# A quantised cross-attention and mixture-of-experts block: rounding on ScalarE, paired maxima, queries stacked before keys

## The reference, cut to what matters

```python
def _qdq(x):                       # symmetric int8, one scale per row
    s = maximum(max(abs(x), axis=-1) / 127, 1e-8)
    return clip(round(x / s), -127, 127) * s

q = _qdq(layernorm(x)) @ _qdq(wq).T + bq
k, v = split(ctx @ wkv.T + bkv, 2)
attn = softmax(q @ k.T / sqrt(32))            # 16 heads, 512 x 1601 each
o = attn @ v
x = x + tanh(g0) * (_qdq(o) @ _qdq(wp).T + bp)
x = x + tanh(g1) * moe(layernorm(x))          # 32 experts, top 4, capacity 128,
                                              # plus a shared SwiGLU
```

## Time and profile before

| | |
|---|---|
| runs of the kernel, median (lowest to highest) | 3401.5 us (3399.94 to 3410.48) |
| the profiled execution | 3410.04 us, of which the span is 3408.1 us |
| mean granted TensorE clock | 0.912 of full speed |
| PE busy | 2915.5 us, 86% |
| DVE / ACT / POOL busy | 1958.9 us (57%) / 1265.7 us (37%) / 1826.3 us (54%) |
| setup and first maxima | 0 to 137 us |
| attention | 137 to about 2691 us |
| SwiGLU and routing | about 2691 to 3160 us |
| experts | 3160 to 3408 us |

### The profile page before, as it was taken

One profiled execution on the slowest core, in us unless ns is written; L12 is line 12 of the kernel. 1 busy time (PEld: TensorE's weight loads), 2 busy tenths in 40 slices (PEclk: granted clock), 3 DMA queues, 4 the chain that ended last, 5 costly groups with the idle time before them and its releaser, 6 DMA issues. The chain is left out here.

```text
span 3408.1 us, 43422 instructions
## 1 busy us (share of the span) xinstructions
PE 2915.5 (86%) x14836; PEld 1224.1 (36%) x14876; DVE 1958.9 (57%) x4052; ACT 1265.7 (37%) x2268; POOL 1826.3 (54%) x1570
## 2 busy tenths in 40 slices
PE   5997888888888887988798879888989879998787
PEld 3233333333333332333233333333333334443665
DVE  7667566756675667567666766675566143434122
ACT  2254435443544354445444534454345410100111
POOL 0285566456645575556465646564658613233555
PEclk9798999799979998998899979997999789999899
DMA  4111012110211031102110211121110221131897
GB/s 126 27 42 49 24 28 71 45 35 17 79 36 37 17 92 35 39 12 89 33 33 20 85 31 32 34 74 28 32 45 20 75 87 53 60 111 49 249 288 193
DMA packets 146651, 215.73 MB, mean 63 GB/s; under 512 B 25016, under 2 KB 78264, under 8 KB 146432
## 3 DMA queue, kind: packets, MB, share of 16 engines
q1 hardware_dynamic: 130560, 196.08, 19.1%
q0 software_dynamic: 15872, 16.87, 2.6%
HBM read 126.62 MB, written 34.37 MB: 47 GB/s over the span
## 5 line engine op out<-in xcount | busy, mean ns | idle before, releaser
L1439 POOL TENSOR_TENSOR prob_acc<-prob_acc,probs 128x512 f32<-128x512 f32 x1152 | 1449.4, 1289 | 614.4 <-ACT probs L965 614.1
L965 ACT ACTIVATE probs<-s_ps 128x512 f32<-128x512 f32 (+1 forms) x1664 | 942.9, 596 | 1091.6 <-PE s_ps L786 1060.9
L1184 DVE TENSOR_REDUCE piece_max<-r_ps 128x1 f32<-128x400 f32 (+1 forms) x2048 | 1025.2, 565 | 176.0 <-PE r_ps L708 172.6
L708 PE MATMUL r_ps<-k_flat,q_stack 96*128 96x400 f16 (+1 forms) x2048 | 637.4, 366 | 238.8 <-DVE piece_max L1184 138.2
L786 PE MATMUL s_ps<-q_stack,k_flat 97*128 97x512 f16 (+1 forms) x1664 | 649.8, 407 | 64.7 <-ACT probs L965 57.0
L800 PE MATMUL o_ps<-probs,v_sb 128*32 128x512 f32 (+1 forms) x3328 | 480.2, 651 | 19.8 <-ACT probs L965 19.8
L708 PEld LDWEIGHTS r_ps<-k_flat,q_stack 96*128 96x128 f16 x2048 | 205.1, 101 | 556.0 <-DVE piece_max L1184 268.4
L786 PEld LDWEIGHTS s_ps<-q_stack,k_flat 97*128 97x128 f16 (+1 forms) x1664 | 163.8, 103 | 645.6 <-ACT probs L965 389.6
L1436 POOL COPY prob_acc<-probs 128x512 f32<-128x512 f32 x128 | 72.8, 612 | 520.2 <-PE sum_ps L820 383.7
L1471 POOL DMA_INDIRECT slot_rows<-payload,slot x128 | 125.3, 979 | 315.0 <-DVE slot L1369 192.8
L1178 DVE SCALAR_TENSOR_TENSOR k_lo<-r_ps,bk_col,k_hi 128x400 f16<-128x400 f32 (+1 forms) x128 | 81.8, 639 | 333.2 <-ACT k_hi L923 333.2
(11 more groups left out here) (190 smaller groups left out, 2781.2 us busy)
## 6 DMA issues: line engine op xcount, KB each, us to landing
k_flat<-k_hi SPq DMA_DIRECT2D x256, 100.1 KB, 2.2
ctx_raw<-in_ctx SPq DMA_DIRECT2D x96, 256.0 KB, 2.7
v_sb<-in_L_ffn_w SPq DMA_DIRECT2D x48, 512.0 KB
xin<-in_x SPq DMA_DIRECT2D x16, 1024.0 KB, 5.5
k_flat<-k_lo SPq DMA_DIRECT2D x128, 100.1 KB, 2.2
ctx_hi<-in_L_ffn_w SPq DMA_DIRECT2D x24, 512.0 KB
ctx_lo<-in_L_ffn_w SPq DMA_DIRECT2D x24, 512.0 KB
q_stack<-q_hi SPq DMA_DIRECT2D x256, 32.0 KB, 1.9
```

Source lines behind the costliest of these rows:

```text
L708: last = nc.tensor.matmul(ps[:, 0:w], q_stack[0:KSPLIT, g % 2, j, qt * P:(qt + 1) * P], k_stack[0:KSPLIT, g % 2, j, at:at + w], start=True ...
L965: nc.scalar.activation(probs[0:w, slot, j, :], s_ps[j % SBANKS][0:w, :], ACT.Exp).then_inc(probs_ready, 1)
L1184: V.reduce_max(piece_max[:, j * TT + qt, i:i + 1], ps[:, 0:PIECE[i]], X_AXIS).then_inc(free_of(*key), 1)
L1439: last = G.tensor_tensor(prob_acc[:, j, :], prob_acc[:, j, :], probs[:, slot, j, :], ALU.add)
```

## The change

It has five parts.

1. **Normalising and rounding move to ACT.** `normalised` becomes `Identity(x * rstd + shift)`, `rounded` `Identity(x * inv + 12582912)`, `integers` subtracts it into bf16. VectorE keeps one pass, a clip between the last two, with both bounds. Two tiles go in a step. For x the statistics move to step 1, the deviation to 2, the scale stays at 6. For h, h_ready comes from ACT at steps 3 and 4.
2. **Maxima in pairs.** A `"max"` tile is now two matmuls into two neighbouring banks, read by one reduction over 2 x 401 or 2 x 400 columns. A pair starts at an even bank; where the tile before ended on an even one, a bank is skipped.
3. **Queries before keys** also where g=0: the `q` tile moves from step 1 to the lead of step 0, ahead of the first key piece, and SP copies queries first everywhere but at the very start.
4. **The row of maxima** goes by one DMA from `max_row` to `q_stack`.
5. At the start `x` is loaded after the first context tile, not the third.

```diff
-X_STATS, X_STD, X_NORM, X_SCALE, X_QUANT = 2, 3, 4, 6, 7
-O_SCALE, O_QUANT, O_TURN, Y_AT = 3, 4, 9, 10
-H_STATS, H_STD, H_NORM, LATE_HEADS = 0, 1, 2, 10
+X_STATS, X_STD, X_RSTD, X_NORM, X_SCALE, X_ROUND, X_CLIP, X_INT = 1, 2, 3, (4, 5), 6, (7, 8), (8, 9), (10, 11)
+O_SCALE, O_ROUND, O_CLIP, O_INT, O_TURN, Y_AT = 3, (4, 5), (5, 6), (7, 8), 9, 10
+H_STATS, H_STD, H_RSTD, H_NORM, LATE_HEADS = 0, 1, 2, (3, 4), 10
...
-    return (x_tiles(nb) if ng == 0 else [("q", nb, ng)]) + key_tiles(nb, ng)[0:2]
+    return (x_tiles(nb) if ng == 0 else []) + [("q", nb, ng)] + key_tiles(nb, ng)[0:2]
...
+        for key in order:
+            wide = 2 if key[0] == "max" else 1
+            at += at % wide
+            banks = [(at + i) % NBANKS for i in range(wide)]
+            at += wide
...
             def stacks(b, g):
 
-                if g == 0:
+                if (b, g) == (0, 0):
                     stack_keys(b, g, range(GH))
...
                 sp.wait_ge(max_row_ready, group(b, g) + 1)
-                sp.dma_start(max_scr[g % 2], max_row[:, :]).then_inc(max_out, DMA)
-                sp.wait_ge(max_out, (group(b, g) + 1) * DMA)
                 sp.dma_start(q_stack[KSPLIT:KSPLIT + 1, g % 2, :, :].rearrange("o j n -> o (j n)"),
-                             max_scr[g % 2].rearrange("(o a) n -> o (a n)", o=1)).then_inc(max_in, DMA)
+                             max_row[:, :]).then_inc(max_in, DMA)
...
+                    w = MAX_WIDE[i]
+                    open_tile(*key)
+                    for ps, at in zip(r_ps[ring.bank(*key):], MAX_AT[i]):
+                        last = nc.tensor.matmul(ps[:, 0:w], q_stack[0:KSPLIT, g % 2, j, qt * P:(qt + 1) * P],
+                                                k_stack[0:KSPLIT, g % 2, j, at:at + w], start=True, stop=True)
...
+            def normalised(dst, tiles, ready, count, done):
+
+                act.wait_ge(ready, count)
+                for t in tiles:
+                    nc.scalar.activation(dst[:, t, :], xin[:, t, :], ACT.Identity, scale=rstd[:, t:t + 1],
+                                         bias=shift[:, t:t + 1]).then_inc(done, 1)
+
+            def rounded(src, tiles, ready, count, done):
+
+                act.wait_ge(ready, count)
+                for t in tiles:
+                    nc.scalar.activation(src[:, t, :], src[:, t, :], ACT.Identity, scale=inv[:, t:t + 1],
+                                         bias=rounder[:, 0:1]).then_inc(done, 1)
+
+            def integers(src, tiles, ready, count, done):
+
+                for t in tiles:
+                    act.wait_ge(ready, count + t + 1)
+                    nc.scalar.activation(q_int[:, t, :], src[:, t, :], ACT.Identity, bias=rounder[:, 1:2]).then_inc(done, 1)
...
+            def clip_rows(src, tiles, ready, count, done):
+
+                for t in tiles:
+                    dve.wait_ge(ready, count + t + 1)
+                    V.tensor_scalar(src[:, t, :], src[:, t, :], ROUND + 127.0, ROUND - 127.0, ALU.min, ALU.max).then_inc(done, 1)
...
+                    full(dve, *key)
+                    k = ring.bank(*key)
+                    V.reduce_max(piece_max[:, j * TT + qt, 2 * i:2 * i + 2], r_all[:, k:k + 2, 0:MAX_WIDE[i]], X_AXIS
+                                 ).then_inc(free_of(*key), 1)
```

More of the change, by code:

```diff
@@ L34 @@
 PIECE_AT = [sum(PIECE[:i]) for i in range(PIECES)]
+PAIRS = PIECES // 2
+MAX_WIDE = [max(PIECE[2 * i:2 * i + 2]) for i in range(PAIRS)]
+MAX_AT = [(PIECE_AT[2 * i], PIECE_AT[2 * i + 1] + PIECE[2 * i + 1] - MAX_WIDE[i]) for i in range(PAIRS)]
 E, TOPK, EGROUPS, EPG, CAP, F, FS = 32, 4, 4, 8, 128, 256, 512
@@ L84, in max_tiles @@
 def max_tiles(b, g):
-    return [("max", b, g, j, qt, i) for j in range(GH) for qt in range(TT) for i in range(PIECES)]
+    return [("max", b, g, j, qt, i) for j in range(GH) for qt in range(TT) for i in range(PAIRS)]
 def x_tiles(b):
@@ L432, in full @@
         def full(eng, *key):
-            k = ring.bank(*key)
-            eng.wait_ge(bank_full[k], ring.done(*key))
-            return r_ps[k]
+            eng.wait_ge(bank_full[ring.last_bank(*key)], ring.done(*key))
+            return r_ps[ring.bank(*key)]
         def free_of(*key):
-            return bank_free[ring.bank(*key)]
+            return bank_free[ring.last_bank(*key)]
         def wait_read(eng, *key):
@@ L560, in ffn_in @@
                     key = ("hT", f - 2, DC - 1)
-                    sp.wait_ge(bank_full[ring.bank(*key)], ring.done(*key))
+                    sp.wait_ge(bank_full[ring.last_bank(*key)], ring.done(*key))
                     sp.wait_ge(out_written, (f - 1) * DMA)
@@ L606, in open_tile @@
             def open_tile(*key):
-                k = ring.bank(*key)
-                if ring.uses_before(*key):
-                    pe.wait_ge(bank_free[k], ring.uses_before(*key))
-                return r_ps[k]
+                for k, count in ring.before[key]:
+                    pe.wait_ge(bank_free[k], count)
+                return r_ps[ring.bank(*key)]
             def close(last, *key):
-                last.then_inc(bank_full[ring.bank(*key)], 1)
+                last.then_inc(bank_full[ring.last_bank(*key)], 1)
             pe.wait_ge(consts_ready, 1)
@@ L1001, in _ @@
                 tile(key)
+            for at in O_ROUND + O_INT:
+                o_part(B - 1, at)
             for f in range(B):
@@ L1131, in h_part @@
                     variances(h_var_ready)
-                elif at == H_NORM:
-                    inverse_std(h_std_ready, b + 1)
-                    for t in range(TT // 2):
-                        step.mark(normalised(work, t))
-                elif at == H_NORM + 1:
-                    for t in range(TT // 2, TT):
-                        last = normalised(work, t)
-                        if t < TT - 1:
-                            step.mark(last)
-                    last.then_inc(h_ready, 1)
+                elif at == H_RSTD:
+                    inverse_std(h_std_ready, b + 1, h_rstd_ready)
             def tile(key):
@@ L1232, in _ @@
             heads_out(B - 1, GROUPS - 1)
-            quantise(work, so).then_inc(o_quantised, 1)
+            for at in (O_SCALE,) + O_CLIP:
+                o_part(B - 1, at)
             def scores_in_groups():
@@ L1483, in gather @@
                 key = ("ey", e - UN) if e >= UN else ("down", B - 1, TT - 1)
-                pool.wait_ge(bank_full[ring.bank(*key)], ring.done(*key))
+                pool.wait_ge(bank_full[ring.last_bank(*key)], ring.done(*key))
                 step.carry_wait()
```

142 lines of the change are left out of this document (87 added, 55 removed).

## The result

| | before | after |
|---|---|---|
| median of the runs (lowest to highest) | 3404.01 us (3399.94 to 3410.48) | 3250.49 us (3247.85 to 3254.07) |
| ratio, 95% interval | | 0.9548 (0.9529 to 0.9567) |
| the profiled execution, its span | 3410.04, 3408.1 | 3254.07, 3251.4 |
| mean granted TensorE clock | 0.912 | 0.950 |
| PE / DVE / ACT busy, us | 2915.5 / 1958.9 / 1265.7 | 2811.8 / 1727.0 / 1387.3 |

The account below looks back on a forecast made before the run. PE was taken to bound attention, stopped mainly by VectorE at the maxima and returning at half clock. Terms 66 + 140 + 30 + 1 = 237 us off 3410 gave 3173, forecast as 3170; main case 3110 to 3240, range 3090 to 3300.

Parts of the forecast that it names:

- Pairs: Attention's maxima: one reduction over two banks saves 0.08 us a pair, seen in 20 groups and the start; about 30 us.
- The bound of -60: Lower bound for maxima in pairs: each remaining stop 0.45 us longer, and a bank skipped beside every single tile.
- The passes: Normalising and rounding off VectorE: 182 us gross, less 21 for clips and 21 on ACT; about 140 us.
- ScalarE's share, 21: The moved passes' cost on ACT, behind a step's fourth exponential: 3 us a batch, 21 in all; at worst 97.
- my 2.55 against 2.5: Before a step's first exponential ACT needs 2.55 us while PE has about 2.5 us of work: just covered, except in g=2.
- Queries first: Queries copied before keys in g=0: PE starts g=3's first query earlier, 9.4 us in each of 7 batches, 66 us.
- The rest: Direct copy of the maxima row and later h_ready in SwiGLU, with SwiGLU and experts unchanged: together +1 us.
- Statistics one step earlier: Statistics of x moved ahead of step 3: no gain, since PE then waits for a context tile; -3 to +3 us a batch.
- the one that ended slower: Rival: with two pair places PE and VectorE take turns, 3640 us; signs: reductions 0.98 us or more, over 40 waits; chance 0.05.
- ScalarE takes VectorE's place: Rival: uncovered ACT bursts hold PE, 3310 us; sign: `s_ps` waits for ACT above 15 us a batch; chance 0.13.
- The change does little: Rival: VectorE's stops return at the next maxima, 3320 us; sign: g=2 still near 90 us; chance 0.09.
- Everything goes: Rival: the clock stays up and stops at the scales shrink too, 20 us a batch more, 3090 us; chance 0.11.

Follow-up runs that it names:

- run 10: The kernel before with queries first and the direct copy of the maxima row; single maxima, all normalising and rounding on VectorE: 3358.44 us, ratio 0.9842.
- run 1: The changed kernel with maxima taken one bank at a time again, all else as changed: 3181.28 us, ratio 0.9323.
- run 6: The kernel with single maxima (3181 us), but the ring still skips a bank where a pair would have to: 3218.77 us, ratio 0.9439.
- run 7: The kernel with single maxima (3181 us), with the row of maxima sent through DRAM again: 3175.75 us, ratio 0.9303.
- Runs 9 and 11: 9: single-maxima kernel without ScalarE's square root, 3169.97 us. 11: single maxima, row maxima in halves, four context-tile places in place of three, 3121.6 us.
- run 8: The kernel with single maxima (3181 us), with the row maxima of x and o taken in two halves, one a step earlier: 3142.19 us, ratio 0.9218.

## Why the forecast was 80 us too low

The sum was 66 + 140 + 30 + 1 = 237. The measured 154 us are parted by the ratios in the same way: 54 for the order with the direct copy (before to run 10), 177 for the passes (run 10 to run 1), -77 for the pairs (run 1 to the changed kernel). By the medians as they stand the pairs are -69, because the kernel before was 8 us slower beside the runs than beside the changed kernel; I go on with 69, the smaller. (237 off the runs' own 3401.5 would have been 3165, not 3170; that is within the noise.)

**Pairs: the step that failed, 99 us of the sum.** "20 groups x 1.3, and 3 at the start, 29 in all" looked only at what the instruction saves. That part was too small: 49 us were measured. The other side stood beside it as the lower bound, "a pair gives its banks back only when both are read", "and a bank is skipped beside every single tile", and was not priced into the value taken. The runs show that it costs 37 + 81 = 118 us. The bound of -60 was not low enough either, since I charged the late return only to stops that already stood in the profile; the pairs made new ones, 28 a batch for 9 in run 1 with single maxima. The clock is not what was lost: it was 0.950 over the program for 0.948 in run 1, and PE is busy 7 us longer and idle 63. The Trainium skill, "TensorE: Matmul & The Clock Gate", "A second HAM failure mode", tells of a clock that swings because of short idles in a bank cycle. The short idles are there in the trace, but between run 1 and the changed kernel no clock was lost; of the runs between them run 6 alone shows longer busy time, at 0.943.

**The passes: 177 for 140.** The stops went as told: `piece_max` fell from 19.7 us a batch in run 10 to 5.9 in run 1, 13.8 where the sum had 14. (Of the six stops behind these passes five, and not six, are of 2 us or longer; the sixth is 1.63.) PE's idle time fell by 10.2 only, since waits for other things grew, that for a context tile by 1.8. Three sizes were off. The clock gave back 16.5 us of PE's busy time a batch, the loss by the clips already taken off, where 12 were taken. The clips cost 35 for 21. And ScalarE's share, 21, does not show: PE waits 6.8 us a batch for the exponentials in run 10 and 6.7 in run 1. ScalarE's passes are even longer than the 0.60 us I took from a row that reads PSUM (forms of after, ns min/median/max):

```profile
L942 ACT ACTIVATE xin<-xin,rounder,inv x32: 799/808/816, 59.2 to 2172.4; 128x512 f32<-128x512 f32 x32
...
L949 ACT ACTIVATE q_int<-xin,rounder x32: 708/718/728, 63.8 to 2189.2; 128x512 bf16<-128x512 f32 x32
```

So "it is just covered" was right by the result, but not by my 2.55 against 2.5: with the measured lengths the first would be 3.0. Why the cover is wider was not tried.

**Queries first: 53 to 56 for 66.** The mechanism is as told: the first query copy goes out long before the last `k_lo`, and PE starts 3.46 us after that has ended (SP, VectorE and PE in g=3 of after):

```profile
1583.10 1.15 SPq L517 DMA_DIRECT2D q_stack<-q_hi  x2
```

```profile
1594.40 0.64 DVE L1246 SCALAR_TENSOR_TENSOR k_lo<-r_all,bk_col,k_hi 128x400 f16<-128x400 f32 x1 [2.93 <-ACT k_hi L996]
```

```profile
1598.50 0.52 PE L732 MATMUL r_all<-k_flat,q_stack 96*128 96x401 f16 x2 [1.34 <-DMA k_flat<-k_hi]
```

But that `k_lo` ends 18.4 us into the group, and I had 17.2 us ("at about 1688"). PE starts 21.9 us into it for 28.6, so 6.7 us are gained and not 7.7. The granted clock of g=3 is 1.00, where it was 0.94.

**The rest.** The direct copy gives nothing that can be told from zero (run 7; 1 us was taken). Statistics one step earlier and the earlier load of x were not tried alone. Runs 9 and 11 show that the wait for a context tile behind the statistics is real: four places take it away and give 21 us.

**The rivals.** Of the one that ended slower, the mechanism is in the result: by its own mark, reductions at 0.98 us or more (986 ns), it is there, by the other, over 40 waits a batch, not fully (28). It costs 69 us, not 470; that a pair in flight and PE's other work cover the rest is my reading and was not tried. (Its 3640 also leaves the 30 us of pairs in; with them out it is 3670.) "ScalarE takes VectorE's place" is refuted by its own mark: 15 us a batch of waits for ScalarE were asked for, and it is 7.8 in the changed kernel. "The change does little" falls by g=2. "Everything goes" was half right for the scales: their stops can be cut (run 8), but don't go by themselves. Its price was also mistaken: 20 us a batch more would be about 3020, and 3090 needs only some 10. The measured 3250 lies in none of the cases as priced, above the 3110 to 3240 of the main one and below the two near 3310 and 3320; it is in the range because that was drawn wider, and because the passes gave 37 us more than taken while the pairs gave 99 less. That these two misses partly cancel is luck.

## What to carry to other kernels

A wider instruction that takes two buffers at a time has two prices: what it saves on the engine that reads, and what the ring loses on the engine that fills. Price the second with all other users of the ring, also where the profile shows no stop yet. In this kernel, where two engines take turns at four buffers, the finer hand-over was worth more than fewer instructions (run 1), and the long instruction ahead of it was best cut in halves (run 8). Look at the whole program before you call a cost idle time or clock: one batch hid the clock in run 6 and in run 8.

## What the runs showed of the hardware

A VectorE instruction need not be large to be slow beside GpSimd. The scale over 128x4 numbers takes 171 ns at its fastest, at 59 us, where GpSimd has nothing to do. The other seven stand in g=2, and the median of the eight is 1198; in batch 4 GpSimd then adds nine 128x512 tiles without a break in 11.1 us (forms of run 1):

```profile
L1107 DVE TENSOR_SCALAR sx<-amax x8: 171/1198/1205, 59.0 to 2098.1; 128x4 f32<-128x4 f32 x8
```

The reduction just ahead of it, over 128x2048 numbers, takes 2275 to 2277 ns in all eight places.

ScalarE's passes from SBUF, by contrast, spread over some 20 ns only (799 to 816 and 708 to 728), with and without GpSimd beside them. With a scale and a bias for each row they take 0.81 us, with a bias alone 0.72, and an exponential of the same width from PSUM, with neither, 0.60. It need not be SBUF that costs: the pass that makes `k_hi` reads PSUM too, has a bias for each row, and takes 598 ns for 400 columns only. Source and row operands were not tried apart.

And changing its function for the square root shows as a row of its own, 1283 ns, 16 times (and 15 times back for the exponential). The exponentials follow it at once. That is 40 us, of which the run without it got back 11:

```profile
L928 ACT ACT_TABLE_LOAD  x16: 1283/1283/1283, 48.3 to 2514.3; - x16
```
